# Experts' second products in 16-bit parts: from eight of sixteen to twelve, with high parts on a second engine

## The reference, cut to what matters

```python
x = _layernorm(x + _L0_attn_ref(x, ...))
x = _layernorm(x + _L0_xattn_ref(x, ctx_1024, ctx_1024, ...))     # exp of 16 x 128 x 77 scores per sequence
x = _layernorm(x + _L0_ffn_ref(x, ...))

# inside _L0_ffn_ref: every expert is computed for every token, then weighted
def body(acc, expert):
    w1e, b1e, w2e, b2e, ce = expert
    hmid = jax.nn.gelu(x @ w1e + b1e, approximate=False)          # 128 -> 256 channels
    return (acc + (hmid @ w2e + b2e) * ce[:, None], None)         # 256 -> 128 channels
out, _ = jax.lax.scan(body, jnp.zeros_like(x), (w1, b1, w2, b2, c.T))
```

## Time and profile before

| | us |
|---|---|
| median of three runs | 627.86 |
| lowest and highest of them | 626.38, 630.57 |
| the profiled execution, whole | 629.56 |
| its span, first to last instruction | 627.1 |
| its mean granted TensorE clock, share of full | 0.975 |
| busy: PE, DVE, ACT, POOL | 593.1, 418.9, 406.3, 242.9 |

### The profile page before, as it was taken

How to read it: one execution, slowest core, us unless ns; L and a number is a source line. 1 busy time by engine, 2 the same in 40 slices (tenths; PEclk the granted TensorE clock), 3 DMA queues, 4 the chain that set the end, 5 groups by cost and what they waited for, 6 DMA issues and landing times. The chain is left out here.

```text
span 627.1 us, 16585 instructions
## 1 busy us (share of the span) xinstructions
PE 593.1 (95%) x6513; PEld 434.3 (69%) x6513; DVE 418.9 (67%) x1472; ACT 406.3 (65%) x519; POOL 242.9 (39%) x166
## 2 busy tenths in 40 slices
PE   7898979999999999999999999999999998999994
PEld 3644735787677876877677867786777866676664
DVE  2457377666777778678868677678767775365445
ACT  2337536885559765885669655975678657965651
POOL 5336413443344426163434334342525342234342
PEclk9897698999999999999999999999999999999998
DMA  7622020010200120011100210012000110000000
GB/s 175 190 77 70 26 61 14 20 29 11 60 22 2 46 70 19 4 46 40 50 3 2 63 54 19 4 45 71 19 3 19 29 44 4 19 1 2 1 18 18
DMA packets 31541, 23.05 MB, mean 37 GB/s; under 512 B 2744, under 2 KB 30152, under 8 KB 31464
## 3 DMA queue, kind: packets, MB, share of 16 engines
q1 hardware_dynamic: 23801, 16.59, 9.0%
q10 hardware_dynamic: 7311, 4.97, 2.7%
q0 software_dynamic: 352, 0.43, 0.5%
HBM read 13.90 MB, written 5.46 MB: 31 GB/s over the span
## 5 line engine op out<-in xcount | busy, mean ns | idle before, releaser
L717 ACT ACTIVATE g<-ps,b 128x512 f32<-128x512 f32 x256 | 168.1, 685 | 86.3 <-PE ps L1004 85.1
L536 POOL TENSOR_TENSOR gl<-g,gh 128x1024 f16<-128x1024 f32 x64 | 138.3, 2160 | 212.3 <-ACT gh L706 212.3
L1363 DVE SCALAR_TENSOR_TENSOR acc<-ps,cw,acc 128x128 f32<-128x128 f32 x448 | 125.4, 342 | 103.0 <-PE ps L1027 57.3
L1027 PEld LDWEIGHTS ps<-w,g 128*128 128x128 f32 x1024 | 121.6, 192 | 9.8 <-issue 4.6
L1027 PE MATMUL ps<-w,g 128*128 128x128 f32 x1024 | 127.0, 277 | 0.2
L1002 PE MATMUL ps<-x2h,w1h 128*128 128x512 f16 x256 | 98.0, 383 | 8.9 <-ACT g L717 8.1
L1003 PE MATMUL ps<-x2l,w1h 128*128 128x512 f16 x256 | 97.7, 382 | 0.0
L1004 PE MATMUL ps<-x2h,w1l 128*128 128x512 f16 x256 | 97.5, 381 | 0.0
L1023 PE MATMUL ps<-w2h,gh 128*128 128x128 f16 x512 | 89.2, 219 | 1.7 <-DVE acc L1363 1.5
L1025 PE MATMUL ps<-w2h,gl 128*128 128x128 f16 x512 | 89.0, 219 | 0.0
L1024 PE MATMUL ps<-w2l,gh 128*128 128x128 f16 x512 | 89.0, 219 | 0.0
(11 more groups left out here) (188 smaller groups left out, 869.3 us busy)
## 6 DMA issues: line engine op xcount, KB each, us to landing
q_rep<-q_parts SPq DMA_DIRECT2D x24, 128.0 KB
x<-in_x SPq DMA_DIRECT2D x8, 256.0 KB, 3.2
w_stage<-in_L_ffn_w ACTq DMA_DIRECT2D x1, 2048.0 KB, 13.2
q_swap<-q SPq DMA_DIRECT2D x16, 128.0 KB, 2.1
q_parts<-qx SPq DMA_DIRECT2D x16, 128.0 KB, 1.7
k_rep<-k_parts SPq DMA_DIRECT2D x24, 77.0 KB
out<-fin SPq DMA_DIRECT2D x7, 256.0 KB, 2.5
k_parts<-kx SPq DMA_DIRECT2D x8, 154.0 KB, 2.1
```

Source lines behind the costliest of these rows:

```text
L536: pool.tensor_tensor(gl[:, j % SPLIT_RING, :, :], g32[:, e % RING, :, :], gh[:, j % SPLIT_RING, :, :], ALU.subtract).then_inc(s["lo"], 1)
L717: act.activation(g32[:, e % RING, h, :], bH[:, h, :], ACT.Gelu, bias=b1[:, e, h:h + 1], scale=1.0 / WS).then_inc(s["gelu"], 1)
L1027: m = pe.matmul(o, g32[:, e % RING, h, tok], w2[:, j, h, :], start=(h == 0), stop=(h == HALF - 1))
L1363: m = dve.scalar_tensor_tensor(out=(acc_all if e == E - 1 else acc)[:, b, :], in0=second_bank(f, e)[:, b * P:(b + 1) * P], scalar=cw[:, b, ...
```

## The change

`SPLIT` grows from the eight odd experts to the twelve whose number is no multiple of four; `WHOLE` keeps 0, 4, 8 and 12. The rings `gh` and `gl` grow to three. Experts 2, 6, 10 and 14 get their high part from DVE (`BY_VECTOR`), the other eight of `SPLIT` from ACT as before. Each exp is issued as two, over two PSUM banks each, and `scores_t` fills the two pairs of banks one after the other, each waiting only for its own half of the exp before. A one-column exp (`warm_exp`) stands ahead of the very first one. The second weights come in four loads of four experts, and seven parts instead of six are split. Some semaphores are merged. All tables of places are drawn anew.

```diff
-SPLIT = tuple(range(1, E, 2))
-WHOLE = tuple(range(0, E, 2))
-SPLIT_RING = 2
+SPLIT = tuple(e for e in range(E) if e % 4)
+WHOLE = tuple(range(0, E, 4))
+SPLIT_RING = 3
+BY_VECTOR = tuple(range(2, E, 4))
+BY_SCALAR = tuple(e for e in SPLIT if e not in BY_VECTOR)
...
-DVE_AT = dict(q=11, kv01=5, kv23=25, k_rot=25, k_mean=27, kv=30, den=31, out=36, norm1=37, norm2=39, x1=51,
+DVE_AT = dict(high=3, q=24, kv01=6, kv23=16, k_rot=25, k_mean=22, kv=30, den=33, out=36, norm1=37, norm2=42,
...
-PE_FILL0 = dict(q=2, kv01=12, kv23=0, k_mean=0, kv=0, den=0, out=2, v1=0, k=10, x1_t=50, q_x=1)
+PE_FILL0 = dict(q=9, kv01=8, kv23=7, k_mean=3, kv=0, den=0, out=0, v1=7, k=0, x1_t=49, q_x=0)
...
-HIGH_W = (28, 67, 73, 77, 77, 85)
+HIGH_W = (50, 59, 73, 74, 75, 76, 86)
...
             def low(f, e):
                 j = SPLIT.index(e)
-                since(pool, "hi", len(SPLIT) * f + j + 1)
+                if e in BY_VECTOR:
+                    since(pool, "hi_ve", len(BY_VECTOR) * f + BY_VECTOR.index(e) + 1)
+                else:
+                    since(pool, "hi", len(BY_SCALAR) * f + BY_SCALAR.index(e) + 1)
...
                     if p == at["scores_t"][b]:
-                        since(act, "t_p", n + 1)
-
+                        if n == 0:
+                            act.activation(warm_exp[:, :], xbq[:, :], ACT.Exp)
                         since(act, "av_p", n - 1)
                         act.wait_ge(s["i_wl"], 4)
-                        act.activation(prob[:, b % 2, :].rearrange("p (r n) -> p r n", r=4), ps[0:CTX, 0:4, :],
-                                       ACT.Exp, scale=float(HD) ** -0.5).then_inc(s["prob"], 1)
+                        for half in range(2):
+                            two = slice(2 * half, 2 * half + 2)
+                            since(act, "t_p", 2 * n + half + 1)
+                            act.activation(prob[:, b % 2, :].rearrange("p (r n) -> p r n", r=4)[:, two, :], ps[0:CTX, two, :],
+                                           ACT.Exp, scale=float(HD) ** -0.5).then_inc(s["prob"], 1)
...
-                since(pe, "prob", n)
-                for i in range(BLK):
-                    for r in range(4):
-                        m = pe.matmul(ps[0:CTX, r, i * P:(i + 1) * P], k_rep[32 * r:32 * r + 32, i, b * CTX:(b + 1) * CTX],
-                                      q_rep[32 * r:32 * r + 32, i, b * P:(b + 1) * P], start=True, stop=True)
-                m.then_inc(s["t_p"], 1)
+                for half in range(2):
+                    since(pe, "prob", 2 * (n - 1) + half + 1)
+                    for i in range(BLK):
+                        for r in (2 * half, 2 * half + 1):
+                            m = pe.matmul(ps[0:CTX, r, i * P:(i + 1) * P], k_rep[32 * r:32 * r + 32, i, b * CTX:(b + 1) * CTX],
+                                          q_rep[32 * r:32 * r + 32, i, b * P:(b + 1) * P], start=True, stop=True)
+                    m.then_inc(s["t_p"], 1)
...
+            def high(f, e):
+
+                j = SPLIT.index(e)
+                since(dve, "gelu", HALF * (E * f + e + 1))
+                if j >= SPLIT_RING:
+                    since(dve, "y_p", E * f + SPLIT[j - SPLIT_RING] + 1)
+                else:
+                    since(dve, "y_p", E * (f - 1) + SPLIT[j - SPLIT_RING] + 1)
+                dve.tensor_copy(gh[:, j % SPLIT_RING, :, :], g32[:, e % RING, :, :]).then_inc(s["hi_ve"], 1)
```

More of the change, by code:

```diff
@@ L79, in constants @@
     return np.ascontiguousarray(np.concatenate(list(cols.values()), axis=1), np.float32), where
[L84 to L88, removed]
@@ L89 @@
-DVE_AT = dict(q=11, kv01=5, kv23=25, k_rot=25, k_mean=27, kv=30, den=31, out=36, norm1=37, norm2=39, x1=51,
[L90 to L95, removed]
+PE_AT = dict(x_t=2, q=4, kv01=5, kv23=14, k_mean=22, kv=32, den=34, out=36, cx_t=43, v1=44, x1_t=60, k=50,
+             q_x=63, scores=(5, 10, 10, 13, 14, 18, 20, 21), max_t=26, scores_t=(30, 35, 38, 40), values=(38,
+             40, 41, 43), wo=54, x2_t=62, logits=0, c_t=57, b2=62, first=3, next=0, second=0, u_t=(43, 48),
+             ao_t=51)
@@ new lines @@
+ACT_AT = dict(x_t=0, q=6, kv23=17, cx_t=42, x1_t=60, k=51, q_x=63, max_t=25, scores_t=(31, 38, 39, 40), x2_t=61,
+              weights=0, c_t=58, gelu=1, high=3, u=(40, 42), ao_t=51)
+DVE_AT = dict(high=3, q=24, kv01=6, kv23=16, k_rot=25, k_mean=22, kv=30, den=33, out=36, norm1=37, norm2=42,
+              x1=51, v1=45, k=52, q_x=63, scores=(5, 9, 9, 13, 15, 20, 20, 22), max=23, pairs=(44, 46), wo=53,
+              x2=58, x2_t=61, logits=0, weights=2, cw=10, b2=61, combine=0, finish=50, q_sin=25, sums=32, xl=0,
+              cw_hl=41)
@@ L100 @@
+PE_ONE = dict(x_t=0, q=0, kv01=0, kv23=10, k_mean=12, kv=18, den=18, out=22, cx_t=42, v1=44, k=51, x1_t=49,
               q_x=63)
[L101 to L111, removed]
@@ L119 @@
[L119 to L122, removed]
-FILL_START = 17
-PE_FILL0 = dict(q=2, kv01=12, kv23=0, k_mean=0, kv=0, den=0, out=2, v1=0, k=10, x1_t=50, q_x=1)
-PE_FILL1 = dict(q=8, kv01=5, kv23=0, scores=0, max_t=1, scores_t=4, kv=11, den=0, out=0, k_mean=7, values=0,
-                wo=3, q_x=1, x2_t=0, v1=0, x1_t=15, u_t=43)
@@ L129 @@
-HIGH_W = (28, 67, 73, 77, 77, 85)
-LOW_W = (33, 67, 90, 91, 116, 126)
-SCALE_W = (49, 105)
-LOAD_W = (25, 26, 45, 74)
-W1_W = (7,)
-ROWS_W = (16, 11)
+PE_ZERO = dict(x_t=0, q=4, kv01=11, kv23=17, k_mean=19, kv=25, den=29, out=30, cx_t=39, v1=54, x1_t=57, k=56,
+               q_x=63, scores=(3, 3, 7, 10, 11, 14, 18, 18), max_t=20, scores_t=(25, 29, 31, 37), values=(32,
+               34, 38, 39), wo=54, x2_t=61, logits=1, c_t=47, b2=56, first=2, next=0, second=2, u_t=(39, 46),
+               ao_t=51)
@@ L1428, in body @@
                             cross(g, p)
+                        if f is not None and p % PLACES == at["high"] and e in BY_VECTOR:
+                            high(f, e)
                         if f is not None and p % PLACES == at["combine"]:
```

124 lines of the change are left out of this document (69 added, 55 removed).

## The result

The changed kernel takes 624.6 us (median of 22 runs, 622.0 to 628.7) where the kernel before, run beside it, takes 628.8 (22 runs). The ratio is 0.9938, with a 95% interval of 0.9925 to 0.9951: 0.6% faster, 4 us. The forecast was 611.5 us, a gain of 16.5; about a quarter of it came, and the time lies outside the range of 604 to 621. The profiled span fell from 627.1 to 622.7 us.

What follows compares the result with a forecast made beforehand. PE was taken to bound the full bodies. The profiled 629.56 us, less 14.1 for second products and 2.4 for the start, gave 613.1; the median was put at 611.5 us, range 604 to 621.

Steps and rivals of the forecast that it cites:

- all on PE, which bounds a full body, so I count it whole: Step that counted the second products' 14.1 us in full as time saved.
- There PE is the bound and nearly without holes: Reading of a full body: PE busy 67.41 of 68.5 us at clock 1.00.
- Second products: Four more experts split in eight groups: 0.43 us each, 0.51 in the last group, 14.1 us gained on PE.
- Redrawn places: Only the start's redrawing was priced, bounded by 6 us gained and 4 lost; full bodies' places had no term.
- low parts on POOL were hidden: Four more low parts of 2.16 us a body, costed at nothing; POOL idles 212.3 us before its low parts.
- High parts on DVE: 32 casts on DVE at 0.69 us, bound 1.23, costed at nothing since DVE idles before combines.
- The rival: DVE casts caught behind POOL's low parts delay combines and PE: 30.4 us lost, 641.8 us, chance 0.06.
- Exps in halves: Two halves cost ACT 0.22 us more an exp; 2.0 us gained and lost, net nothing, bounds 2.5 gained, 12.3 lost.
- The 2.0 us taken as gained on PE's waits for exps: PE idled 2.5 us for whole exps before scores_t; half exps were to save 2.0 us of it.
- The ACT rival: ACT alone sets the exp stretch, so converted seconds gain nothing there: 12.3 us lost, 623.8 us, chance 0.09.
- Its sign: PE idle until a gelu right after a group's last exp, by about a microsecond in each body.
- The start: Earlier x2n transposes and first gelus, less a later cast: 2.4 us gained, bounds 6 gained and 4 lost.

Runs made afterwards that it cites:

- run 18: run 13's kernel with DVE splitting the score maxima ahead of the query's steps, still gelu for exp: 613.9 us, body 67.2.
- run 13: Changed kernel, mostly old places (x2's and the query's redrawn), whole exps, gelu for the softmax's exp, max_t=26 on PE: 613.1 us, body 67.20.
- run 7: Changed kernel with full groups' places as before (plus DVE's high parts) and whole exps: 648.9 us, ratio 1.0321.
- run 9: run 7's kernel with the places of the second norm and of x2's transposes taken from the redrawn tables: 628.9 us, ratio 1.0013.
- run 17: run 14's kernel with DVE splitting the score maxima ahead of the query's steps: 622.8 us, ratio 0.9911.
- run 14: run 13's order with the softmax's exps in place and the exp table loaded early: 621.4 us, ratio 0.9873.
- Run 2: Changed kernel with the high parts of experts 2, 6, 10 and 14 on ACT instead of DVE: 628.9 us, ratio 1.0007.
- run 1: Changed kernel with each exp and each scores_t whole again: 624.0 us, ratio 0.9933.
- run 3: Changed kernel with gelu in place of the softmax's exp, so no table switch: 615.2 us, ratio 0.9786.
- run 4: Kernel before with gelu in place of the softmax's exp, so no table switch: 621.2 us, ratio 0.9874.
- run 5: Changed kernel with a one-column exp ahead of each group's first exp and its waits: 622.8 us, ratio 0.9906.
- run 12: Kernel before with only the changed kernel's tables of the start, first attention and filler: 642.3 us, ratio 1.0242.

## Why the prediction was wrong, point by point

**Sign and kind: right. Size: a quarter.** The step that failed is "all on PE, which bounds a full body, so I count it whole", which rests on "There PE is the bound and nearly without holes"; and, with it, that the sum had no term at all for the redrawn order of the full bodies. In place of 1.7 us a full body fell by 0.10: PE's second products did fall by 1.60, but PE's waits grew by 0.66, its changes of form by 0.62, and the rest by 0.22. PE busy 98% of a body does not say that nothing else is nearly as late. ACT's stretch of exps lies within 1 us of it, and so does DVE's stretch around the score maxima in the old order (9.53 of 10 us in run 18).

**Second products (14.1 us).** Right as a price: 1.60 us in a full body after, 1.66 in run 13, against 1.72; 3.3 in bodies 0 and 1 together, without idle time, against 3.44. But in a full body 0.66 came back as waits, 0.62 as changes of form, 0.22 as the rest. In the last group, where nothing else stands on PE, 2.7 us came against 2.1 (four times 0.51 is 2.04): behind its `x2n` transposes stand five products that changed form, not four, since the second products lag behind.

**Redrawn places, costed at nothing outside the start.** Wrong both ways. They cost PE 0.62 us a body in changes of form, and they are worth 20 us where they take POOL's `rstd` from behind a low part (runs 7 and 9). I had said that low parts on POOL were hidden, since POOL idles 212 us before them. That idle time was POOL waiting at a low part, with whatever stands behind it in the queue waiting too; at the old places that was `rstd`. I never asked what else is queued on POOL.

**High parts on DVE (0.69, bound 1.23, hidden).** The price is right: 0.684 us, all four of a full body between 683 and 693 ns. The rival's mechanism is real too, and the order decides where it shows: in the changed kernel one of the 32 casts took 1.40 us beside a POOL step; in runs 17 and 18 one in each full body took 1.53, beside `kr`, and in runs 13 and 14 one took 1.10. None was caught behind a low part, where the rival had put them. Run 2 shows the casts worth 4.3 us, since ACT is relieved.

**Exps in halves (0.22 us an exp, net nothing).** Two halves take 1.93 in a row against 1.87; the net was nothing (run 1). The 2.0 us taken as gained on PE's waits for exps did not come: they grew from 2.5 to 4.3 us. The ACT rival was not about halves. Its mechanism, a stretch that ACT sets, is real, as runs 3, 4 and 5 show, and its 623.8 us is close to the 624.6. Part of that is chance: it priced all seven bodies, changes of form and the start not at all. Its sign, a wait of PE right behind the last exp, did not come either; the waits stand inside the stretch, 0.50 us for a gelu and 0.43 for an exp. I gave it 0.09 because ACT has 1.0 us free there. Of that, 0.71 lay in front of gelus, whose first products PE had not done yet (0.34 at 400.11 and 0.37 at 412.74):

```profile
400.11 1.33 ACT L717 ACTIVATE g<-ps,b 128x512 f32<-128x512 f32 x2 [0.34 <-PE ps L1004]
```

In the changed kernel 0.54 lay in front of a table load, waiting for `scores_t`, and became of use only when the load was issued ahead of that wait (run 5).

**The start (2.4 us gained, bounds 6 and minus 4).** Up to the end of body 1 the trace shows 1.0 us gained in all, where the sum had 2.4 and two bodies' 3.4; and up to 1.7 us of what it shows there can be the clock, as said with the result. `x2n` is ready at 89.6 instead of 86.9. The wait of 2.1 us for the first gelus has gone, as forecast, and one for the query's DMA stands in its place:

```profile
95.10 0.46 PE L929 MATMUL ps<-k_rep,q_rep 32*128 32x77 f16 x16 [1.49 <-DMA q_rep<-q_parts]
```

Which part of the start makes `x2n` late was not tried further; run 12 could not separate it from the weight loads.

**What stays open.** Whether some order reaches 66.3 us a body without table switches (67.91 less 1.6), which is what the sum amounts to there. None here got under 67.2 even without table switches, and each wait taken away was followed by another: DVE's maxima, DVE's combines.

## What to carry to other kernels

An engine at 98% of a body is relieved only down to the next chain, and a new order can cost it time of its own. Before a gain on it is counted whole, look at windows of 10 to 20 us for a second engine over 95%, and ask for each stretch what comes free when the first engine arrives earlier. For an operation that is added to an idle engine, list what stands behind it in its queue: idle time that ends on a semaphore inside a queue is not free for those behind. And a table load that stands behind its instruction's wait can be had earlier with a one-element instruction of the same table ahead of that wait.
